# Spreading per-head scalars over partitions: products with a head mask, or 32x32 block transposes

## The chip, the cores and the metric

The kernel runs on one core of a Trainium2 chip. The metric is the device time of the whole program in microseconds (us). The engines are TensorE (PE in the profile; PEld is its weight load), VectorE (DVE), ScalarE (ACT), GpSimd (POOL) and SyncE (SP), each with its own stream of instructions that it runs in order, with waits on semaphores between them.

## The reference, cut to what matters

```python
# x: (64, 32, 512), ctx: (64, 257, 512), 16 heads of 32 columns
x = x + cross_attention(layernorm(x), ctx) @ W_out.T + b_out   # keys = values = ctx
x = x + self_attention(layernorm(x), ...)                      # 16 heads, rope, 32 keys
x = x + moe_ffn(layernorm(x), ...)                             # one of 8 experts a token
# cross attention, for each batch and head:
sim  = q @ k.T * 32 ** -0.5            # 32 queries x 257 keys
out  = softmax(sim) @ v                # = (exp(sim - max) @ v) / sum(exp(sim - max))
```

257 keys are two blocks of 128 and one key more. The kernel takes the two blocks with TensorE and adds the last key by hand: its probability times its value row. It divides by the sums after that, on the attention's result.

## The kernel before, in words

The 64 batches are taken one after the other, each in 11 steps (`STEPS`). Four batches with their 32 queries make a tile of 128 rows; a tile is 44 steps (`TILE`), and there are 16 tiles. Every engine's program is one loop `for step in range(LAST_STEP)`. In a step it issues first its part of the batch now in work (scores, maxima, exponentials, transposes of the probabilities, products with the values, transposes of the next keys), by `step % 11`, and then, in `stages(step)`, the parts of the tiles already past, at the offsets written out by hand at the top of the file. `tile_at(step, offset)` says for which tile a stage is due; offset 0 is the first step after the tile's fourth batch. An offset only fixes the place in the engine's order: the time comes from the waits.

So at each tile boundary (steps 0 to 13 of a tile) work of three tiles meets the first batch `b` of the next one. The order on each engine, by step, is in the kernel before:

- **VectorE**: copy of transposed probabilities of the batch before (step -3), `TURN_K + 1` copies into `k_block` (-2), `X2` add with layernorm statistics of an older tile (1), `largest(b, 0)` and `largest(b, 1)`, the maxima of the scores (2), `SOFT` maximum and subtraction of self-attention (2), `ATT`: last key's product and the sum with `att_bank` (3), `ATT_INV`: product with one over the sums (4), `turn_keys` for `b + 1` (5, 7), `SOFT_SUM` (6), `SOFT_TURN` (12), `largest` of `b + 1` (13), `turn_keys` for `b + 2` (16), `X1` add (17).
- **ScalarE**: `SCALE3`, layernorm of the older tile, which waits for the `X2` statistics (-2), four exponentials of batch `b` (2), `SOFT_EXP` (2), `ATT_HI` (4), copy of transposed probabilities (6).
- **GpSimd**: `PLACE_INV` (-5), `PLACE_LAST` (0), the root for the older tile's layernorm (1), `ATT_LO` (2), `SOFT_SCALE` (4), `keep_last` and `move_last` (7, 9), which place the last key of batch `b + 1`.
- **TensorE**: scores of `b` (0), `attend(b - 1, 1)` and `SELF` (1), `SPREAD` and `SPREAD_INV` (3), `turn_prob(b, 0)` (6), `TURN3` (7), `turn_prob(b, 1)` (8), `attend(b, 0)` (10), `XOUT` in four parts (10 to 13), scores of `b + 1` (11), `attend(b, 1)` (12), `turn_prob(b + 1, 0)` (17), `QKV` (from 24).

The attention result lies in `att_bank` with head dimensions on partitions and the queries of four batches along the columns. The probabilities of the last key (`plast`) and one over the sums (`inv`) lie the other way: a head and a query on a partition, one column for a group of heads and a batch. To bring them over, GpSimd multiplies them into a 0/1 pattern (`latent`), 128x512, and TensorE multiplies four 128x128 blocks of that with a 0/1 mask `samehead`. These results are in two banks of PSUM, which other stages use before and after.

A fp32 product stands as two records in the trace. `XOUT` multiplies operands cut in two (`operand_hi`, `operand_lo`), which `ATT_HI` on ScalarE and `ATT_LO` on GpSimd make from `att_w`.

In the set-up the weights are prepared in units between the first batches. VectorE waits there for a DMA of tables, then copies them, `samehead` among them in 16 copies, at step `TABLES_AT`.

Of the kernel before, what the change touches and what calls it, by code (L numbers as in the profile page):

```python
# [10 lines left out]
P = 128  # L11
# [27 lines left out]
(INVERT, PLACE_LAST, PLACE_INV, X_BIAS, SPREAD, SPREAD_INV, ATT, ATT_INV, ATT_HI, ATT_LO, XOUT, X1, SCALE1, TURN1, QKV, OUT_BIAS, TURN_Q, TURN_K,  # L39
 SELF, SOFT, SOFT_EXP, SOFT_SUM, SOFT_SCALE, SOFT_TURN, SOFT_PLACE, AV, OUT, X2, SCALE3, TURN3, GATE, CHOOSE, RANK,  # L40
 QUERIES) = (
    -5, 0, -5, -6, 3, 3, 3, 4, 4, 2, 10, 17, 19, 21, 24, 26, 41, 41, 45, 46, 46, 50, 48, 56, 55, 63, 83, 89, 86, 95, 105, 105, 118, -54)
# [44 lines left out]
TABLES_AT = 17  # L87
BIAS_LOAD_AT = 8
# [14 lines left out]
def constant_table():  # L103
# [11 lines left out]
        "latent": (p[:, None] % S == np.arange(S)[None, :]),  # L115
        "ofbatch": (p[:, None] // S == np.arange(BT)[None, :]),
# [3 lines left out]
        "samehead": (p[:, None] // HD == p[None, :] // HD),  # L120
# [54 lines left out]
def program(nc, ins, out, const_at, x2_dram, norm3_dram):  # L175
# [37 lines left out]
    ident, latent, rope = const("ident"), const("latent"), const("rope")  # L213
    samehead = sba("samehead", [P, G, HL, HD])
    last_t = sba("last_t", [P, G, B])
# [16 lines left out]
    op_plast = late[:, 5, :].rearrange("p (g b i) -> p g b i", g=G, b=BT)  # L232
# [42 lines left out]
    op_inv = staged_c[:, 0, :].rearrange("p (g b i) -> p g b i", g=G, b=BT)  # L275
# [29 lines left out]
    def pairs(t_):  # L305
# [26 lines left out]
    inverted, plast_placed, inv_placed, spread_done, inv_spread, spread_used, att_added, att_used = (  # L332
        signal(n) for n in ("inverted", "plast_placed", "inv_placed", "spread_done", "inv_spread", "spread_used", "att_added", "att_used"))
# [36 lines left out]
    bank_of = {"queries": 0, "spread": 0, "xout": 0, "norm": 1, "qkv0": 1, "qkv2": 1, "out": 2, "inv": 1, "gate": 0, "av": 0, "qkv1": 2, "q": 1, "k": 0, "norm3": 1, "rank": 0, "qkv3": 0, "self": 1}  # L370
    step_of = {"queries": QUERIES, "spread": SPREAD, "inv": SPREAD_INV, "xout": XOUT, "norm": TURN1, "qkv0": QKV, "qkv1": QKV + 4, "qkv2": QKV + 8, "qkv3": QKV + 12,
# [6 lines left out]
    emptied = {"queries": queries_placed, "spread": spread_used, "inv": att_used, "xout": x1_made, "norm": norm_lo, "q": q2_moved, "self": soft_shifted, "av": self_lo,  # L378
# [26 lines left out]
    def sync_program():  # L405
# [41 lines left out]
        a, b = const_at["latent"][0], const_at["rope"][1]  # L447
        sp.dma_start(consts_1[:, :], ins["const"][:, a:b]).then_inc(tables_loaded, 16)
        a, b = const_at["before"][0], const_at["samehead"][1]
# [39 lines left out]
    def tensor_program():  # L489
# [64 lines left out]
        def attend(b, pair):  # L554
# [5 lines left out]
            for gg in range(2):  # L560
                for c in range(C2):
                    g = 2 * pair + gg
                    for hl in range(HL):
                        place, at, h = hl ^ g, g * P + bl * S, hl * G + g
                        done = pe.matmul(att_bank[hl * HD:(hl + 1) * HD, at:at + S], context[b % 4][:, c, h * HD:(h + 1) * HD],  # L565
                                         prob_t[pair][:, gg, c, place * S:(place + 1) * S], start=(c == 0), stop=(c == C2 - 1))
            done.then_inc(attended, 1)

        def set_up(n):
# [4 lines left out]
            else:  # L574
                until.wait_ge(last_ready, 1)
            if n in units_of_bank[1]:
                until.wait_ge(queries_placed, 2)
            if kind == "xout":
                until.wait_ge(staged_a_loaded, 16)

                for o in range(G):
                    for hl in range(HL):
                        h = hl * G + c
                        done = pe.matmul(bank[hl * HD:(hl + 1) * HD, o * P:(o + 1) * P], staged_a[:, o, h * HD:(h + 1) * HD], ident, start=True, stop=True)
# [21 lines left out]
            if kind == "bias":  # L606
                until.wait_ge(tables_made, 3)
# [9 lines left out]
        def stages(step):  # L617
# [3 lines left out]
            t = tile_at(step, SPREAD)  # L621
            if t >= 0:
                bank = bank_for("spread", t)
                until.wait_ge(tables_made, 3)
# [1154 lines left out]
```

## Time and profile before

| | |
|---|---|
| time, median of 3 runs | 858.45 us (856.07 to 860.0) |
| span of the profiled execution | 854.9 us |
| median less span | 3.55 us |
| busy share of TensorE, VectorE, ScalarE, GpSimd | 90%, 71%, 49%, 37% |
| distance of two boundaries | 36.4 us (15 in 546.5 us, from 70.9 to 617.4) |

The profiled execution has no time of its own beside its span; what lies around the span is taken as the 3.55 us of the table. A busy share is a mean over stages with different limits. An engine that is late at one boundary is late for all that is queued behind it.

### The profile page before, as it was taken

Reading aid. Unit: us, or ns where it says so; the run is one execution under the profiler, and the core shown is the slowest. Engines: PE = TensorE matmul, PEld = TensorE weight load, DVE = VectorE, ACT = ScalarE, POOL = GpSimd, SP = SyncE. Lnnn points to the kernel's source line nnn. Section 1 sums busy time; section 2 is a strip of 40 time slices with the busy share of each in tenths; the row PEclk is TensorE's granted clock in tenths of the full one; section 3 lists DMA queues with packets and bytes.
Section 4 is the critical chain, followed back from the end, with each engine's and each line's share of the span. In section 5 each row is a group of like instructions: output and inputs, shape, how many; then the busy total and the mean of one; then the engine's idle time right before and its main releaser. Section 6 shows DMA issues by size and latency. Waiting matters only on the chain.

```text
span 854.9 us, 26663 instructions
## 1 busy us (share of the span) xinstructions
PE 768.7 (90%) x10666; PEld 577.6 (68%) x10666; DVE 610.8 (71%) x1211; ACT 422.9 (49%) x1062; POOL 313.9 (37%) x638
## 2 busy tenths in 40 slices
PE   4897979989899898988989899898988789999998
PEld 3544767768676786867768676786876556666664
DVE  3477677777877768787777877778645557788883
ACT  2353464554645556464554645546322354555552
POOL 2013533333234242333233234243220435876642
PEclk9999999999999999999999999999999899999999
DMA  9955654656646565484554636564061499454430
GB/s 277 331 130 100 132 153 118 143 140 130 153 112 160 124 162 138 100 184 120 148 142 117 163 110 152 128 159 101 3 222 51 140 375 388 163 172 140 144 115 3
DMA packets 113850, 129.16 MB, mean 151 GB/s; under 512 B 13951, under 2 KB 80767, under 8 KB 113729
## 3 DMA queue, kind: packets, MB, share of 16 engines
q1 hardware_dynamic: 105984, 109.35, 47.7%
q0 software_dynamic: 5520, 16.26, 5.6%
q10 hardware_dynamic: 2224, 1.86, 0.8%
q8 instruction: 85, 1.39, 0.7%
q14 instruction: 37, 0.30, 0.1%
HBM read 114.85 MB, written 14.42 MB: 151 GB/s over the span
## 4 chain that ended last, share of the span: by engine, by line
PE 61%; DVE 16%; POOL 7%; issue 6%; ACT 4%; DMA 3%; SPq 3%; DVEq 0%; POOLq 0%
PE bank L500 10%; PE bank L1560 8%; PE bank L502 8%; PE bank L501 8%; PE bank L494 4%; PE scores L541 3%; PE scores L551 3%; PE bank L565 2%; PE scores L1538 2%; PE scores L1540 2%; PE scores L1539 2%; DVE negmax L1031 2%; PE bank L605 2%; POOL soft L1315 2%; POOL operand_lo L1292 2%
## 5 line engine op out<-in xcount | busy, mean ns | idle before, releaser
L826 ACT ACTIVATE prob<-scores,negmax 128x257 f32<-128x257 f32 x256 | 118.2, 477 | 42.0 <-DVE negmax L1031 41.3
L500 PE MATMUL bank<-qkv_hi,operand_hi 128*128 128x396 f32 x256 | 99.3, 388 | 4.3 <-DVE operand_lo L1035 4.2
L1031 DVE TENSOR_REDUCE negmax<-scores 128x2 f32<-128x514 f32 x128 | 82.1, 683 | 22.2 <-PE scores L541 22.2
L1021 DVE STREAM_TRANSPOSE k_t<-keys 128x512 f32<-128x512 f32 x128 | 88.3, 691 | 5.6 <-DMA keys<-in_ctx 5.5
L501 PE MATMUL bank<-qkv_lo,operand_hi 128*128 128x396 f32 x256 | 88.1, 344 | 0.0
L502 PE MATMUL bank<-qkv_hi,operand_lo 128*128 128x396 f32 x256 | 87.8, 343 | 0.0
L1560 PE MATMUL bank<-w_all,hidden 128*128 x184 | 82.8, 592 | 0.6 <-ACT hidden L1613 0.6
L551 PE MATMUL scores<-consts,prob 128*128 128x128 f32 x512 | 77.6, 276 | 1.6 <-ACT prob L826 1.6
L565 PEld LDWEIGHTS bank<-prob_t,context 128*32 128x32 f32 x4096 | 47.0, 113 | 42.9 <-issue 34.9
L1656 DVE TENSOR_TENSOR w_lo<-w_all,w_hi 128x512 fp32r<-128x512 f32 x89 | 73.3, 882 | 0.2
L551 PEld LDWEIGHTS scores<-consts,prob 128*128 128x128 f32 x512 | 63.2, 144 | 9.6 <-ACT prob L826 2.5
L1026 DVE COPY prob_t<-scores 128x512 f32<-128x512 f32 x64 | 43.0, 672 | 29.4 <-PE scores L551 29.4
L565 PE MATMUL bank<-prob_t,context 128*32 128x32 f32 x4096 | 59.5, 200 | 4.0 <-ACT prob_t L816 3.3
L1560 PEld LDWEIGHTS bank<-w_all,hidden 128*128 128x128 f32 x184 | 34.7, 189 | 35.6 <-issue 33.9
L541 PE MATMUL scores<-k_t,q_t 32*32 32x257 f32 x2048 | 54.0, 395 | 5.4 <-POOL k_t L1265 5.4
L500 PEld LDWEIGHTS bank<-qkv_hi,operand_hi 128*128 128x128 f32 x256 | 48.5, 189 | 13.2 <-DVE operand_lo L1035 6.2
L1592 ACT ACTIVATE w_hi<-w_all 128x512 fp32r (+1 forms) x92 | 54.4, 640 | 5.6 <-PE scores L1540 3.4
L876 ACT ACTIVATE soft_block<-late 32x512 f32<-32x512 f32 x60 | 37.7, 628 | 34.5 <-DVE late L1149 33.4
L826 ACT ACTIVATION_READ_ACCUMULATOR prob<-scores,negmax 128x1 f32 x256 | 52.5, 205 | 0.0
L501 PEld LDWEIGHTS bank<-qkv_lo,operand_hi 128*128 128x128 f32 x256 | 48.8, 191 | 0.0
L502 PEld LDWEIGHTS bank<-qkv_hi,operand_lo 128*128 128x128 f32 x256 | 48.4, 189 | 0.0
L816 ACT ACTIVATE prob_t<-scores 128x512 f32<-128x512 f32 x64 | 37.7, 589 | 15.1 <-PE scores L551 14.7
(249 smaller groups left out, 1705.5 us busy)
## 6 DMA issues: line engine op xcount, KB each, us to landing
keys<-in_ctx SPq DMA_DIRECT2D x256, 128.0 KB, 4.4
context<-in_ctx SPq DMA_DIRECT2D x64, 512.0 KB, 4.6
w_all<-in_L_ffn_W SPq DMA_DIRECT2D x16, 1024.0 KB, 12.3
b<-in_L_ffn_b SPq DMA_DIRECT2D x23, 256.0 KB, 3.6
norm_scratch<-norm SPq DMA_DIRECT2D x16, 256.0 KB, 2.0
x_tile<-in_x SPq DMA_DIRECT2D x8, 256.0 KB, 4.9
x_pair<-in_x SPq DMA_DIRECT2D x8, 256.0 KB, 4.7
x_scratch<-x_tile SPq DMA_DIRECT2D x8, 256.0 KB, 2.5
```

The costliest lines, as they stand in the source:

```text
L500: pe.matmul(to, op_hi[op][:, c, :], w_hi[name][:, c, columns], start=(c == 0), stop=False)
L501: pe.matmul(to, op_hi[op][:, c, :], w_lo[name][:, c, columns], start=False, stop=False)
L502: return pe.matmul(to, op_lo[op][:, c, :], w_hi[name][:, c, columns], start=False, stop=(c == G - 1))
L541: done = pe.matmul(scores[place * S:(place + 1) * S, 2 * pair + gg, 0:J], q_t[rows, 2 * pair + gg, bl, :], k_t[pair][rows, gg, :], start=T ...
L551: done = pe.transpose(scores[:, 2 * pair, at:at + P], prob[pair][:, gg, c * P:(c + 1) * P], ident)
L565: done = pe.matmul(att_bank[hl * HD:(hl + 1) * HD, at:at + S], context[b % 4][:, c, h * HD:(h + 1) * HD], prob_t[pair][:, gg, c, place * S ...
L826: act.activation(prob[pair][:, gg, :], scores[:, g, 0:J], ACT.Exp, bias=negmax[b % 2][:, g:g + 1], accum_out=sums[t % 2][:, g, bl:bl + 1]) ...
L1021: dve.transpose(dst, src).then_inc(keys_turned, 1)
L1031: dve.tensor_reduce(negmax[b % 2][:, 2 * pair:2 * pair + 2], scores[:, 2 * pair:2 * pair + 2, 0:J], AX.X, ALU.max, negate=True).then_inc(m ...
L1560: done = pe.matmul(bank[:, :], hidden[s % 2][:, m, :], w_of[:, bass.ds(place, 1), 1, m, :].rearrange("p a n -> p (a n)"), start=(m == 0), ...
L1592: act.activation(w1_hi[:, k, :], weights[:, k, :], ACT.Copy).then_inc(w1_cut, 1)
L1656: dve.tensor_tensor(w1_lo[:, k, :], weights[:, k, :], w1_hi[:, k, :].bitcast(F32), ALU.subtract).then_inc(w1_low, 1)
```

## The change

The spread is made by VectorE's transpose of 32x32 blocks. Its source is `inv` (or `plast`) with each column repeated 32 times; the transpose turns 32 queries on partitions into 32 columns, the same on all 32 partitions of a head. The two patterns, the masks, the eight products for a tile and their two uses of PSUM banks go. The head order of `att_bank` changes with it (`place` in place of `hl`), and so the weight columns of `XOUT`; the last keys' values are wanted in that order too, as `last_p`, which 16 small products and a ScalarE copy at the start make. The product with the last key's value and the product with one over the sums move from VectorE to GpSimd. Offsets: `SPREAD_INV` -3, `SPREAD_LAST` 0 (both VectorE now), `WEIGH_LAST` 1 and `ATT_INV` 3 (GpSimd), `ATT` from 3 to 2, `ATT_LO` from 2 to 4, `XOUT` from 10 to 8.

```diff
-(INVERT, PLACE_LAST, PLACE_INV, X_BIAS, SPREAD, SPREAD_INV, ATT, ATT_INV, ATT_HI, ATT_LO, XOUT, X1, ...
+(INVERT, SPREAD_INV, SPREAD_LAST, WEIGH_LAST, X_BIAS, ATT, ATT_INV, ATT_HI, ATT_LO, XOUT, X1, ...
-    -5, 0, -5, -6, 3, 3, 3, 4, 4, 2, 10, 17, ...
+    -5, -3, 0, 1, -6, 2, 3, 4, 4, 8, 17, ...
# TensorE, attend
-    done = pe.matmul(att_bank[hl * HD:(hl + 1) * HD, at:at + S], ...
+    done = pe.matmul(att_bank[place * HD:(place + 1) * HD, at:at + S], ...
# TensorE, stages
-            t = tile_at(step, SPREAD)
-            if t >= 0:
-                bank = bank_for("spread", t)
-                until.wait_ge(tables_made, 3)
-                until.wait_ge(plast_placed, t + 1)
-                for g in range(G):
-                    done = pe.matmul(bank[:, g * P:(g + 1) * P], samehead[:, g, :, :].rearrange("p h d -> p (h d)"),
-                                     op_plast[:, g, :, :].rearrange("p b i -> p (b i)"), start=True, stop=True)
-                done.then_inc(spread_done, 1)
-            t = tile_at(step, SPREAD_INV)
...
# TensorE, at the start
+            if step == 0:
+                until.wait_ge(last_ready, 1)
+                turn_last(1)
# VectorE, stages
             t = tile_at(step, INVERT)
...
-                until.wait_ge(inv_placed, t)
...
+            t = tile_at(step, SPREAD_INV)
+            if t >= 0:
+                until.wait_ge(inverted, t + 1)
+                until.wait_ge(att_used, t)
+                until.wait_ge(unit_done, UNITS.index(("bias", 1)) + 1)
+                dve.transpose(over_head(inv_t), per_head(inv)).then_inc(inv_spread, 1)
+            t = tile_at(step, SPREAD_LAST)
+            if t >= 0:
+                until.wait_ge(plast_kept, 2 * BT * (t + 1))
+                until.wait_ge(att_added, t)
+                until.wait_ge(unit_done, len(UNITS))
+                dve.transpose(over_head(last_w), per_head(plast[t % 2])).then_inc(last_spread, 1)
             t = tile_at(step, ATT)
             if t >= 0:
-                until.wait_ge(spread_done, t + 1)
-                until.wait_ge(last_ready, 1)
+                until.wait_ge(last_weighed, t + 1)
                 until.wait_ge(att_hi, t)
                 until.wait_ge(att_lo, t)
-                last = last_t[:, :, BT * t:BT * t + BT].unsqueeze(3).broadcast_to([P, G, BT, S])
-                dve.tensor_tensor(grid4(att_w), grid4(banks[bank_of["spread"]]), last, ALU.mult).then_inc(spread_used, 1)
                 until.wait_ge(attended, 2 * (BT * t + BT))
-                until.wait_ge(spread_used, t + 1)
-                dve.tensor_tensor(att_w[:, :], att_w[:, :], att_bank[:, :], ALU.add).then_inc(att_added, 1)
-            t = tile_at(step, ATT_INV)
-            if t >= 0:
-                until.wait_ge(inv_spread, t + 1)
-                until.wait_ge(att_added, t + 1)
-                dve.tensor_tensor(att_w[:, :], att_w[:, :], banks[bank_of["inv"]][:, :], ALU.mult).then_inc(att_used, 1)
+                dve.tensor_tensor(att_w[:, :], last_w, att_bank[:, :], ALU.add).then_inc(att_added, 1)
+        def per_head(t_):
+            return t_[:, :, :].rearrange("p g b -> p (g b)").unsqueeze(2).broadcast_to([P, G * BT, HD])
+        def over_head(t_):
+            return t_.rearrange("p (n i) -> p n i", i=S)
# VectorE, set-up at TABLES_AT
-                for g in range(G):
-                    for hl in range(HL):
-                        from_ = 2 * P + (hl ^ g) * HD
-                        done = dve.tensor_copy(samehead[:, g, hl, :], tables[:, from_:from_ + HD])
# GpSimd, stages (PLACE_LAST and PLACE_INV go)
+            t = tile_at(step, WEIGH_LAST)
+            if t >= 0:
+                until.wait_ge(last_ready, 2)
+                until.wait_ge(last_spread, t + 1)
+                weight = last_p[:, :, BT * t:BT * t + BT].unsqueeze(3).broadcast_to([P, G, BT, S])
+                pool.tensor_tensor(grid4(last_w), grid4(last_w), weight, ALU.mult).then_inc(last_weighed, 1)
+            t = tile_at(step, ATT_INV)
+            if t >= 0:
+                until.wait_ge(inv_spread, t + 1)
+                until.wait_ge(att_added, t + 1)
+                pool.tensor_tensor(att_w, att_w, inv_t, ALU.mult).then_inc(att_used, 1)
```

## Rows read from the trace of the kernel before

**Rows 1.** The page: span, busy time of each engine, chain that ended last.

```profile
span 854.9 us, 26663 instructions
...
PE 768.7 (90%) x10666; PEld 577.6 (68%) x10666; DVE 610.8 (71%) x1211; ACT 422.9 (49%) x1062; POOL 313.9 (37%) x638
...
PE 61%; DVE 16%; POOL 7%; issue 6%; ACT 4%; DMA 3%; SPq 3%; DVEq 0%; POOLq 0%
```

**Rows 2.** Chain over one boundary: start us, length us, what.

```profile
323.06 0.70 DVE x_tile L1158
...
324.62 1.26 DVE negmax L1031 x2
...
329.42 0.64 ACT operand_hi L837
330.13 0.79 POOL operand_lo L1292
...
331.36 1.05 POOL soft L1315
332.80 0.99 PE scores L541 x32
```

**Rows 3.** Groups by line: product pairs (two records each); busy us, mean ns, idle before.

```profile
L627 PE MATMUL bank<-late,samehead 128*128 128x128 f32 x128 | 18.5, 288 | 1.0 <-POOL late L1281 1.0
L635 PE MATMUL bank<-staged_c,samehead 128*128 128x128 f32 x128 | 18.4, 287 | 10.3 <-DVE soft L1132 10.3
```

**Rows 4.** Timeline of that boundary: start us, us, engine line op [idle before <-releaser].

```profile
320.78 0.69 DVE L1026 COPY prob_t<-scores 128x512 f32<-128x512 f32 x1 [1.27 <-PE scores L551]
...
321.65 1.38 DVE L1122 COPY k_block<-bank 32x512 f32<-32x512 f32 x2 [0.18 <-PE bank L494]
...
324.34 1.10 PE L687 MATMUL bank<-k_block,late 128*32 128x128 f32 x32
...
326.06 0.81 ACT L794 ACTIVATE norm<-x_tile,shift_r,rstd_r 128x512 f32<-128x512 f32 x1 [3.03 <-POOL shift_r L1254]
...
328.72 0.64 ACT L868 ACTIVATE soft<-soft 128x512 f32<-128x512 f32 x1
...
330.58 0.46 PE L565 MATMUL bank<-prob_t,context 128*32 128x32 f32 x32
...
331.55 0.47 PE L500 MATMUL bank<-xout_hi,operand_hi 128*128 128x512 f32 x1 [0.50 <-POOL operand_lo L1292]
...
336.52 0.60 PE L551 MATMUL scores<-consts,prob 128*128 128x128 f32 x4
336.72 0.69 DVE L1075 TENSOR_TENSOR x_pair<-x_pair,bank 128x512 f32<-128x512 f32 x1 [1.24 <-PE bank L502]
...
342.68 0.45 PE L500 MATMUL bank<-qkv_hi,operand_hi 128*128 128x396 f32 x1 [0.30 <-DVE operand_lo L1035]
```

**Rows 5.** Groups by line: the VectorE and GpSimd forms nearest to the new ones.

```profile
L1292 POOL TENSOR_TENSOR operand_lo<-late,operand_hi 128x512 fp32r<-128x512 f32 x16 | 20.4, 1274 | 67.3 <-ACT operand_hi L837 67.3
...
L1287 POOL TENSOR_TENSOR staged_c<-inv,consts 128x512 f32<-128x512 f32 x16 | 16.8, 1050 | 70.8 <-DVE inv L1054 70.8
...
L1149 DVE STREAM_TRANSPOSE late<-soft 128x512 f32<-128x512 f32 x16 | 11.4, 712 | 8.4 <-POOL soft L1315 8.3
...
L1065 DVE TENSOR_TENSOR late<-late,bank 128x512 f32<-128x512 f32 x16 | 11.0, 689 | 1.7
```

**Rows 6.** Timeline of the set-up around the tables.

```profile
36.69 1.46 DVE L1225 COPY samehead<-qk 128x32 f32<-128x32 f32 x16
...
39.13 1.37 PE L584 MATMUL bank<-consts,soft_block 128*32 128x128 f32 x32 [3.88 <-DVE xout_lo L964]
```

**Rows 7.** Stretches: busy us of each engine, then granted clock, DMA share, GB/s.

```profile
39.00:42.00 3.00, 2.87 (x66) 2.29 (x67) 3.00 (x6) 0.60 (x1) 0.00 (x0) 0.63 1.07 178
76.50:82.50 6.00, 5.97 (x76) 3.40 (x77) 3.35 (x7) 1.94 (x8) 1.33 (x4) 0.72 0.24 14
331.50:336.50 5.00, 4.63 (x76) 2.94 (x77) 3.13 (x5) 3.24 (x11) 1.40 (x5) 1.00 0.59 98
```

More of the change, by code:

```diff
@@ L38 @@
 TILE = BT * STEPS
-(INVERT, PLACE_LAST, PLACE_INV, X_BIAS, SPREAD, SPREAD_INV, ATT, ATT_INV, ATT_HI, ATT_LO, XOUT, X1, SCALE1, TURN1, QKV, OUT_BIAS, TURN_Q, TURN_K,
+(INVERT, SPREAD_INV, SPREAD_LAST, WEIGH_LAST, X_BIAS, ATT, ATT_INV, ATT_HI, ATT_LO, XOUT, X1, SCALE1, TURN1, QKV, OUT_BIAS, TURN_Q, TURN_K,
  SELF, SOFT, SOFT_EXP, SOFT_SUM, SOFT_SCALE, SOFT_TURN, SOFT_PLACE, AV, OUT, X2, SCALE3, TURN3, GATE, CHOOSE, RANK,
  QUERIES) = (
-    -5, 0, -5, -6, 3, 3, 3, 4, 4, 2, 10, 17, 19, 21, 24, 26, 41, 41, 45, 46, 46, 50, 48, 56, 55, 63, 83, 89, 86, 95, 105, 105, 118, -54)
+    -5, -3, 0, 1, -6, 2, 3, 4, 4, 8, 17, 19, 21, 24, 26, 41, 41, 45, 46, 46, 50, 48, 56, 55, 63, 83, 89, 86, 95, 105, 105, 118, -54)
 MEASURE_X, SCALE_X = 2 * STEPS + 4, 2 * STEPS + 5
@@ L366, in emptied_unit @@
         return {"down": down_moved, "k": k_summed, "bias": bias_moved}[kind], c + 1
-    bank_of = {"queries": 0, "spread": 0, "xout": 0, "norm": 1, "qkv0": 1, "qkv2": 1, "out": 2, "inv": 1, "gate": 0, "av": 0, "qkv1": 2, "q": 1, "k": 0, "norm3": 1, "rank": 0, "qkv3": 0, "self": 1}
-    step_of = {"queries": QUERIES, "spread": SPREAD, "inv": SPREAD_INV, "xout": XOUT, "norm": TURN1, "qkv0": QKV, "qkv1": QKV + 4, "qkv2": QKV + 8, "qkv3": QKV + 12,
+    bank_of = {"queries": 0, "xout": 0, "norm": 1, "qkv0": 1, "qkv2": 1, "out": 2, "gate": 0, "av": 0, "qkv1": 2, "q": 1, "k": 0, "norm3": 1, "rank": 0, "qkv3": 0, "self": 1}
+    step_of = {"queries": QUERIES, "xout": XOUT, "norm": TURN1, "qkv0": QKV, "qkv1": QKV + 4, "qkv2": QKV + 8, "qkv3": QKV + 12,
                "q": TURN_Q, "k": TURN_K, "self": SELF, "av": AV, "out": OUT, "norm3": TURN3, "gate": GATE, "rank": RANK}
@@ L581, in set_up @@
                 for o in range(G):
-                    for hl in range(HL):
-                        h = hl * G + c
-                        done = pe.matmul(bank[hl * HD:(hl + 1) * HD, o * P:(o + 1) * P], staged_a[:, o, h * HD:(h + 1) * HD], ident, start=True, stop=True)
+                    for place in range(HL):
+                        h = (place ^ c) * G + c
+                        done = pe.matmul(bank[place * HD:(place + 1) * HD, o * P:(o + 1) * P], staged_a[:, o, h * HD:(h + 1) * HD], ident, start=True, stop=True)
             if kind == "down":
@@ L606, in set_up @@
             if kind == "bias":
-                until.wait_ge(tables_made, 3)
+                until.wait_ge(tables_made, 2)
                 for k in range(2):
@@ L928, in scalar_program @@
                 load_low()
+            if step == LAST_PLACED_AT:
+                until.wait_ge(last_turned, 2)
+                act.activation(last_p[:, :, :].rearrange("p g b -> p (g b)"), last_bank[:, G * B:2 * G * B], ACT.Copy).then_inc(last_ready, 1)
             if step == BIAS_LOAD_AT:
```

69 lines of the change are left out of this document (23 added, 46 removed).

## The prediction

> **What bounds the kernel now.** I read the page first. It shows TensorE 90% busy and the chain that ended last with only 61% of the span on it [rows 1]. So there are stretches in which TensorE's order waits for the others, and the question is whether the change works in these or in TensorE's own. The groups by line price what goes: the two groups of spreading products have 128 records each, eight in a tile [rows 3]. The chain in order of time places it: from 323.06 to 332.80 us, the boundary between two tiles, it runs over VectorE (`X2` add, statistics, the two maxima, self-attention's maximum and subtraction, the three `ATT` operations), then `ATT_HI`, `ATT_LO`, `SOFT_SCALE`, and back to TensorE with the scores of batch b + 1 [rows 2]. TensorE's own work does not set that stretch. From 342.68 on, when `QKV` starts, it is TensorE's products again. The timeline of the same boundary [rows 4] gives starts and waits. Here VectorE has next to no gap: 1.27 us before the copy at 320.78, 0.18 us before the copies at 321.65, then work without a wait until past 330 us. The boundaries lie 36.4 us apart (the table), so I work out one and count.
>
> **What goes.** On TensorE, eight products a tile, in two groups. Their records overlap, so the busy time counts: 18.5 and 18.4 us over 16 tiles, 1.16 us a group and 2.3 us a tile [rows 3]. To that comes the wait of the second group for the bank that `SOFT` empties, 10.3 us in all, 0.7 in each of 15 boundaries. They are due between the end of `SELF` at 325.44 and `turn_prob(b, 0)`, which waits for exponentials. These start after ScalarE's layernorm at 326.06, which waits 3.03 us for `X2`'s statistics [rows 4]; the four exponentials take from 326.87 to 328.72, 0.46 us each, so two are done at 327.8. The removed products stand in a hole of TensorE that stays; I value them at nothing in the steady boundaries. The bank wait of `TURN3` goes too, and also lies there. GpSimd loses 1.05 us twice, at times when it waits.
>
> **What is added on VectorE.** Before: three operations of 0.69 us, all behind the maxima and `SOFT`. After: two transposes, and one addition of 0.69. A transpose whose source repeats a column is not in the trace. The nearest row is the 128x512 transpose of 0.71 us [rows 5], and I take that. Bounds: 0.25 us a transpose if only the 16 distinct columns counted (my guess at a floor: a third of the row), 1.4 us if the source were taken at half the rate, twice the row. VectorE's total for a tile is the same, but the order isn't. The transpose of `inv` (step -3) stands before the `k_block` copies and finds a gap of 0.18 us, so they come 0.52 us later. The one of `plast` (step 0) stands before the `X2` add and finds none: 0.73 us with its pitch. So `X2` starts at 324.31, not 323.06: 1.25 us later, with the statistics, GpSimd's root, ScalarE's layernorm, the maxima and the exponentials behind it. The addition (step 2) now stands before `SOFT`; VectorE is back at its old time with `turn_keys(b + 1, 0)`, 329.3.
>
> **ScalarE's part.** In the kernel before, two paths ended together at `ATT_HI`: VectorE's third `ATT` operation and ScalarE's `SOFT_EXP`, which ended at 329.36 just before `ATT_HI` at 329.42 [rows 2, 4]. From the layernorm to there ScalarE is without a gap for 3.3 us. The change shortens the first path but shifts the second by the whole 1.25 us, so `ATT_HI` starts at 330.67 and `ATT_LO` at 331.38.
>
> **GpSimd's part.** `WEIGH_LAST` has one operand repeated like `PLACE_INV`: 1.05 us; `ATT_INV` has two full ones like `ATT_LO`: 1.27 us [rows 5]. `WEIGH_LAST` runs from 324.35 to 325.4: the root's statistics come at 325.95 and the addition at 327.15, so it is hidden, with 0.5 us to spare. `ATT_INV` runs from 327.9 to 329.2 and `ATT_HI` is held by ScalarE to 330.67: hidden, 1.4 us to spare. Without that cover it would cost 0.58 us more than on VectorE. The row has 1.27 us on GpSimd for what takes 0.69 on VectorE. The Trainium skill says the same in GPSIMD Reference, Engine selection: elementwise work belongs on VectorE, as GpSimd is about twice as slow with two inputs. By that rule alone the boundary would lose another 0.6 us; by the rows it is cover that decides. `SOFT_SCALE`, `keep_last` and `move_last` are queued behind `ATT_LO`, and come 1.25 us later.
>
> **XOUT earlier in the order.** `ATT_LO` releases `XOUT` at 332.8 (331.55 before). Two of its parts now stand before `attend(b, 0)`, whose operand had been there since about 332, and three before the scores of b + 1. Before, `attend(b, 0)` filled the wait at 330.58, and the stretch from the first part to `turn_prob(b + 1, 0)`, 331.55 to 336.52, held four parts, one `attend` and the scores [rows 4]. After, it holds one `attend` more, 0.46 us of products and some 0.3 of issue, less the 0.3 us that the scores waited for `move_last`: `turn_prob(b + 1, 0)` comes at 338.2. The scores of b + 1 start at about 335.8, not 332.8; VectorE begins their two maxima when the first pair is there, some 0.8 us later (all take 0.99 [rows 2]); the maxima take 1.26, a key transpose 0.7 like the one in [rows 5], and only then comes `X1`, at 338.5. It started at 336.72. From `X1` the chain runs to `QKV` at 342.68 as before. So one boundary costs 1.8 us, of which 1.25 by the transposes' place and 0.5 by the order of `XOUT`. `QKV` and what follows is TensorE's, without slack to win it back.
>
> **The sum.** Thirteen boundaries (t = 2 to 14) have all this work: 13 x 1.8 = 23.4 us. t = 1 has no `X2` behind the transposes: 1.3. The last has no next batch, and only the shift on the way to its `ATT_HI`: 0.8. At t = 0 there is nothing of older tiles: 0. In the set-up the 16 copies, 1.46 us, stand between the tables' landing and the product at 39.13, which waited 3.88 us for them [rows 6]: -1.5. The added 16 products and copy at the start lie before that landing, which waits for nobody's compute: 0. Sum +24.0: a span of 878.9 and, with the 3.55 us around it, 882.5 us. The profiled execution stands for the median, as the table has them.
>
> **The rivals.**
> TensorE is left without work from 325.44 to about 329.1, and again for 1.5 us before `XOUT`. After a wait of 3.88 us in the set-up its granted clock was 0.63 for 3 us, part of it thus at 1.2 GHz [rows 6, 7]. The same stretch of `XOUT`, scores and attends took 6.0 us at 0.72 and 5.0 at 1.00 [rows 7]: 1.0 us more a boundary, 13 us, 895 us. The spreading products had kept TensorE at work there, which speaks for it; against it, the slow time may fall in the second hole. The Trainium skill, TensorE: Matmul & The Clock Gate, Part 1, has the rule that the gate halves the clock after idleness and gives it back after activity. By that rule this rival is the forecast; the traces bear it out in the set-up only. Chance 0.2.
> The transposes are cheap: at 0.25 us, 0.07 + 0.25 and half of the order's 0.5, 0.6 us a boundary: 13 x 0.6 - 1.5 + 1 = +7, 866 us. Chance 0.1.
> No change: their cost is paid by TensorE's relief in parts that I value at nothing, about 858. Chance 0.08.
> The other side: it is TensorE's order that holds the boundary, and the earlier steps only move waits. Then each of 15 boundaries gives 2.3 us of products back, with the set-up 36 us: 822. It decides if the exponentials of b are ready before the removed products would have ended; the 3.03 us wait of the layernorm speaks against it. Chance 0.12, at any size.
> The forecast has 0.5. With transposes at 1.4 us it is 3.1 a boundary, 899.
>
> **Range and chances.** 864 to 899 holds the forecast with its bounds, the clock and the cheap transposes, 0.8. Under 0.5%, 4.3 us, this measurement can't tell from no change. Faster 0.12, same 0.08, slower 0.8. The likeliest's own range is 874 to 890.
>
> **What would show it.** Right: `X2` starts 1.2 us later after the last `out` product; the layernorm's wait on ScalarE grows to over 4 us; a hole of 3.7 us on TensorE before `turn_prob(b, 0)` and one before `XOUT`; `XOUT` still waits for `operand_lo`; boundaries 38.2 us apart, at granted clock 1.00. Wrong: boundaries nearer than 36.4, transposes far from 0.71, a granted clock under 1.00 in the steady part, or GpSimd as what ends VectorE's or ScalarE's waits.

## The result, and the profile after

The changed kernel takes 898.21 us, median of 4 runs (893.85 to 903.07); the kernel before took 858.59 us in 4 runs beside it (856.07 to 860.0). The ratio is 1.0467, interval 1.0418 to 1.0516: slower, by 39.6 us. The forecast was 882.5 us, with a range to 899: the result lies 0.8 us under the end of the range, and outside of the likeliest's own range (874 to 890). The profiled execution took 901.93 us, near the slow end of the four, so the spans below differ by more than the medians, by 45.1 us. Executions that took over 1.5% longer than the fastest of the same kernel are left out of all medians, ranges and ratios here (one of six and two of ten, in two of the experiments).

The page of the changed kernel, lines that answer to [rows 1], and between them TensorE's granted clock in the 40 slices of the span:

```profile
span 900.0 us, 26139 instructions
...
PE 773.6 (86%) x10442; PEld 573.5 (64%) x10442; DVE 604.1 (67%) x1195; ACT 422.1 (47%) x1063; POOL 319.6 (36%) x638
...
PEclk9998898989898898989889898988989889999999
...
PE 55%; DVE 14%; issue 10%; POOL 8%; ACT 7%; SPq 3%; DMA 2%; ACTq 0%; POOLq 0%; DVEq 0%
```

TensorE has 224 instructions fewer than in [rows 1] and is busy 5 us longer: what is left takes longer. Its share of the chain fell from 61 to 55%. The mean granted clock of the execution is 0.926, and the low slices lie all through the steady part.

The same boundary as in [rows 4] (here tile by tile earlier in time, as `X2` at 302.62 us shows), in the timeline of the changed kernel:

```profile
299.88 0.70 DVE L1049 STREAM_TRANSPOSE staged_c<-inv 128x512 f32<-128x512 f32 x1
300.51 1.34 DVE L1114 COPY k_block<-bank 32x512 f32<-32x512 f32 x2
...
301.10 0.40 PE L499 MATMUL bank<-out_hi,operand_lo 128*128 128x512 f32 x1
...
301.88 0.71 DVE L1055 STREAM_TRANSPOSE late<-plast 128x512 f32<-128x512 f32 x1
...
302.62 0.69 DVE L1150 TENSOR_TENSOR x_tile<-x_tile,bank 128x512 f32<-128x512 f32 x1
302.67 1.05 POOL L1273 TENSOR_TENSOR late<-late,last_p 128x512 f32<-128x512 f32 x1 [6.13 <-DVE late L1055]
...
302.83 1.09 PE L667 MATMUL bank<-k_block,late 128*32 128x128 f32 x32
...
305.62 0.81 ACT L781 ACTIVATE norm<-x_tile,shift_r,rstd_r 128x512 f32<-128x512 f32 x1 [4.10 <-POOL shift_r L1248]
...
306.18 1.27 POOL L1278 TENSOR_TENSOR late<-late,staged_c 128x512 f32<-128x512 f32 x1 [0.59 <-DVE late L1062]
...
307.53 1.11 PE L548 MATMUL scores<-consts,prob 128*128 128x128 f32 x4 [3.61 <-ACT prob L813]
...
308.79 0.63 ACT L824 ACTIVATE operand_hi<-late 128x512 fp32r<-128x512 f32 x1
...
309.50 1.28 POOL L1283 TENSOR_TENSOR operand_lo<-late,operand_hi 128x512 fp32r<-128x512 f32 x1 [2.06 <-ACT operand_hi L824]
...
310.83 0.79 PE L497 MATMUL bank<-xout_hi,operand_hi 128*128 128x512 f32 x1 [0.48 <-POOL operand_lo L1283]
...
314.78 0.80 PE L538 MATMUL scores<-k_t,q_t 32*32 32x257 f32 x32
...
317.38 0.65 DVE L1067 TENSOR_TENSOR x_pair<-x_pair,bank 128x512 f32<-128x512 f32 x1
```

The two transposes take 0.70 and 0.71 us. TensorE's last `OUT` product ends at 301.50 and `X2` starts at 302.62, 1.12 us later, since the second transpose stands before it; in the kernel before this is 0.04 us. The layernorm waits 4.10 us (3.03 in [rows 4]). `ATT_INV` on GpSimd (306.18, 1.27 us) ends at 307.45, and `ATT_HI` starts at 308.79: it is covered. `SELF` ends at 303.92, and TensorE then waits 3.61 us for an exponential. The stretches of that boundary (busy us of TensorE, its weight loads, VectorE, ScalarE and GpSimd, then the granted clock, DMA share and GB/s, as in [rows 7]):

```profile
302.00:306.00 4.00, 1.92 (x96) 1.24 (x80) 3.90 (x8) 0.38 (x1) 2.11 (x4) 1.00 0.01 4
306.00:309.00 3.00, 1.47 (x7) 1.47 (x8) 2.00 (x5) 2.97 (x11) 1.27 (x1) 0.57 0.67 187
309.00:312.00 3.00, 2.52 (x10) 1.92 (x9) 2.23 (x5) 1.40 (x3) 2.50 (x5) 0.50 0.99 257
312.00:315.00 3.00, 3.00 (x56) 1.90 (x70) 0.53 (x1) 1.26 (x2) 0.28 (x3) 0.80 0.48 80
315.00:318.00 3.00, 2.50 (x71) 1.34 (x54) 2.45 (x4) 1.72 (x8) 0.00 (x0) 1.00 0.07 16
```

In and after the hole the granted clock is 0.57, 0.50 and 0.80: TensorE has fallen from 2.4 to 1.2 GHz. `XOUT`'s first product takes 0.79 us there (0.47 in [rows 4]); the scores of b + 1 start 12.16 us after `X2` and take 0.80 us, at full clock again.

Where the time went, by the starts of `X2` in the two traces. `X2` of the oldest tile comes at 140.26 before and 145.89 after: +5.6. The 13 distances from there to the last such `X2` sum to 474.89 before (140.26 to 615.15) and 512.52 after (145.89 to 658.41): +37.6, 2.9 a boundary. What follows is 1.9 longer. One distance is 42.90, with a stop that the last section tells of; the other 12 have a mean of 39.1, where the mean was 36.5 before.

### The profile page after: what moved, and what is told of

It reads as the page before. It is cut to its first block, busy times and chain, and to the rows that moved or that the text cites. A ratio compares the mean times of both kernels' runs of the same rounds, so it can differ in the third digit from the quotient of the medians.

```text
span 900.0 us, 26139 instructions
## 1 busy us (share of the span) xinstructions
PE 773.6 (86%) x10442; PEld 573.5 (64%) x10442; DVE 604.1 (67%) x1195; ACT 422.1 (47%) x1063; POOL 319.6 (36%) x638
## 3 DMA queue, kind: packets, MB, share of 16 engines
q1 hardware_dynamic: 105984, 109.26, 46.6%
## 4 chain that ended last, share of the span: by engine, by line
PE 55%; DVE 14%; issue 10%; POOL 8%; ACT 7%; SPq 3%; DMA 2%; ACTq 0%; POOLq 0%; DVEq 0%
PE bank L497 11%; PE bank L498 8%; PE bank L499 8%; PE bank L1551 7%; PE scores L548 3%; PE scores L538 3%; PE bank L562 3%; PE bank L491 3%; ACT prob L813 2%; POOL operand_lo L1283 2%; DVE k_block L1114 2%; PE scores L1529 2%; PE scores L1531 2%; PE scores L1530 2%; PE bank L602 2%
## 5 line engine op out<-in xcount | busy, mean ns | idle before, releaser
L548 PE MATMUL scores<-consts,prob 128*128 128x128 f32 x512 | 89.5, 303 | 60.7 <-ACT prob L813 60.7
L548 PEld LDWEIGHTS scores<-consts,prob 128*128 128x128 f32 x512 | 67.5, 156 | 73.4 <-ACT prob L813 68.1
L1647 DVE TENSOR_TENSOR w_lo<-w_all,w_hi 128x512 fp32r<-128x512 f32 x89 | 69.5, 839 | 0.1
L562 PE MATMUL bank<-prob_t,context 128*32 128x32 f32 x4096 | 61.4, 202 | 1.9 <-issue 1.9
L497 PE MATMUL bank<-xout_hi,operand_hi 128*128 128x512 f32 x64 | 40.7, 635 | 15.4 <-POOL operand_lo L1283 15.4
L863 ACT ACTIVATE soft_block<-late 32x512 f32<-32x512 f32 x60 | 37.7, 628 | 34.1 <-DVE late L1141 33.0
L1265 POOL COPY plast<-prob 128x2 f32<-128x2 f32 x128 | 25.0, 195 | 78.6 <-ACT prob L813 78.6
L538 PE MATMUL scores<-k_t,q_t 32*32 32x257 f32 x2048 | 51.9, 394 | 0.8 <-POOL k_t L1259 0.8
L1273 POOL TENSOR_TENSOR late<-late,last_p 128x512 f32<-128x512 f32 x16 | 16.8, 1050 | 98.9 <-DVE late L1055 98.9
```

The lines of the kernel that those rows point to most:

```text
L497: pe.matmul(to, op_hi[op][:, c, :], w_hi[name][:, c, columns], start=(c == 0), stop=False)
L538: done = pe.matmul(scores[place * S:(place + 1) * S, 2 * pair + gg, 0:J], q_t[rows, 2 * pair + gg, bl, :], k_t[pair][rows, gg, :], start=T ...
L548: done = pe.transpose(scores[:, 2 * pair, at:at + P], prob[pair][:, gg, c * P:(c + 1) * P], ident)
L562: done = pe.matmul(att_bank[place * HD:(place + 1) * HD, at:at + S], context[b % 4][:, c, h * HD:(h + 1) * HD], prob_t[pair][:, gg, c, pla ...
L1647: dve.tensor_tensor(w1_lo[:, k, :], weights[:, k, :], w1_hi[:, k, :].bitcast(F32), ALU.subtract).then_inc(w1_low, 1)
```

## The experiments

All are edits of the changed kernel, but one of the kernel before. Ratios are to the kernel before, run on the same chip beside them. The changed kernel itself was not run again there, so what an experiment gains on it is given as a difference of medians across chips, where the medians of the kernel before lie within 2 us of each other (857.64 to 859.54). "Distance" is that from one `X2` to the next in the one profiled execution, for the same 13 boundaries.

**The order of `XOUT` alone put back** (`XOUT` 8 to 10, so `attend(b, 0)` and the scores of b + 1 stand before its parts as they did).

```diff
-    -5, -3, 0, 1, -6, 2, 3, 4, 4, 8, 17, ...
+    -5, -3, 0, 1, -6, 2, 3, 4, 4, 10, 17, ...
```

> The changed kernel with XOUT back at step 10, so that attend(b, 0) and the scores of b + 1 again stand before its parts two to four; the transposes stay. Theory (place of the transposes 1.25 us, order of XOUT 0.5 us, clock the rest of the 2.9 us a boundary): the order's share comes back, 0.5 to 1.0 us in 13 boundaries, 885 to 892 us, and the clock still falls in the hole before turn_prob(b, 0). Rival (the order of XOUT is what costs, since it holds back the next scores): 865 or less. Rival (order costs nothing once the clock is down): 898.

Measured: 875.62 us, ratio 1.0226 (1.0192 to 1.0260); 22.6 us less than the changed kernel, where the forecast's step had 0.5 a boundary, 6.5 in all. It is between the theory and its rival, and neither holds. Distances are 37.4 to 37.5 in six of 13 tiles, 37.6 to 38.8 in the others; the mean clock rose to 0.949. The clock still fell in every tile, but in nine of them for a shorter time. By the two profiles, 21.3 us of the gain are in the 13 boundaries and 3.8 before the first `X2`. So the order matters more than its products' time at full clock: what it costs and what the clock costs are not separate.

**TensorE's hole filled**: seven products of 256 columns, of constants into a free bank, before `turn_prob(b, 0)`. Their results are used by nobody; nothing else changes.

```diff
# TensorE, stages
+            t = tile_at(step, 3)
+            if 1 <= t:
+                until.wait_ge(qkv_moved, 4 * (t - 1) + 4)
+                for _ in range(7):
+                    pe.matmul(banks[0][:, 0:FILL], ident, consts[:, 0:FILL], start=True, stop=True)
```

> The changed kernel with seven products of 256 columns without use, issued by TensorE at step 3 of each tile from the second on, about 3 us of work in the hole of 3.6 us before turn_prob(b, 0). Theory (the clock falls in that hole and costs 1.0 to 1.3 us a boundary): granted clock 1.00 to 0.98, boundaries 38.2 to 38.4 us apart, 883 to 887 us, although work is added. Rival (the clock falls where it costs nothing and the loss is all late VectorE and ScalarE work): 898 or more.

Measured: 878.79 us, ratio 1.0264 (1.0231 to 1.0297), 19.4 less than the changed kernel (17 to 19 when each is taken against the kernel before beside it), by added work. That is lower than the theory had it. The timeline of a boundary and its stretches:

```profile
215.64 0.69 DVE L1155 TENSOR_TENSOR x_pair<-x_pair,bank 128x512 f32<-128x512 f32 x1
...
216.87 3.29 PE L622 MATMUL bank<-consts 128*128 128x256 f32 x14
...
218.64 0.81 ACT L786 ACTIVATE norm<-x_pair,shift_r,rstd_r 128x512 f32<-128x512 f32 x1 [4.10 <-POOL shift_r L1253]
...
220.55 0.66 PE L548 MATMUL scores<-consts,prob 128*128 128x128 f32 x4 [0.39 <-ACT prob L818]
...
223.85 0.50 PE L497 MATMUL bank<-xout_hi,operand_hi 128*128 128x512 f32 x1 [1.73 <-POOL operand_lo L1288]
```

```profile
216.50:220.50 4.00, 3.66 (x31) 2.75 (x22) 3.93 (x8) 1.84 (x6) 2.56 (x5) 1.00 0.06 20
220.50:223.50 3.00, 1.57 (x12) 1.27 (x12) 1.99 (x5) 2.92 (x8) 0.97 (x1) 1.00 1.00 336
223.50:226.50 3.00, 2.65 (x41) 1.88 (x41) 1.30 (x3) 0.90 (x2) 1.80 (x6) 1.00 0.83 165
```

The hole before `turn_prob(b, 0)` is down to 0.39 us and the clock stays at 1.00. Up to `XOUT` VectorE's, GpSimd's and ScalarE's part is the same to the hundredth (the layernorm again 3.00 us after `X2` and again 4.10 us late), `XOUT` starts 8.21 us after `X2` in both, and `X1` comes 13.7 after it instead of 14.6 to 15.7. The distance is mostly 37.70 (37.67 to 37.88 in eleven tiles); in the two others, of 38.86 and 41.01, the clock fell later in the tile. This run shows the clock's share by itself: some 1.4 us a boundary, 17.8 us in the 13 of them by the two profiles.

**The transpose of `inv` moved to VectorE's gap** (step -3 to -4, where VectorE waits 1.26 us for transposed probabilities before the copy).

```diff
-    -5, -3, 0, 1, -6, 2, 3, 4, 4, 8, 17, ...
+    -5, -4, 0, 1, -6, 2, 3, 4, 4, 8, 17, ...
```

> The changed kernel with the transpose of one over the sums one step earlier (-4), before the copy for which VectorE waited 1.27 us. Theory (its place behind that copy made X2 0.52 us later): X2 starts 0.5 us earlier, 7 us in all, 889 to 892 us with the clock as it is; if the shorter hole also keeps the clock, 880. Rival (a transpose's place does not matter): 898.

Measured: 883.08 us, ratio 1.0302 (1.0242 to 1.0363). The time from the last `OUT` product to `X2` falls from 1.11 to 0.80 us, so this transpose costs 0.31 us there, not the 0.52 of the forecast. The time is under the theory's 889 to 892 and over its 880 for a clock that is kept. Distances are 37.39 in two tiles at clock 1.00, 37.0 to 37.4 in four at 0.95, and 38.4 to 39.5 in six at 0.91; one of 39.29 at clock 1.00 has a stop that the last section tells of. That 0.95 can cost nothing is answered under "Its size" below.

**Both transposes in the gap, and `XOUT`'s order put back** (both at -4; for the first tile `plast`'s stays at step 0).

```diff
-    -5, -3, 0, 1, -6, 2, 3, 4, 4, 8, 17, ...
+    -5, -4, -4, 1, -6, 2, 3, 4, 4, 10, 17, ...
             t = tile_at(step, SPREAD_LAST)
+            if t == 0:
+                t = -1
+            if step == TILE:
+                t = 0
```

> The changed kernel with both transposes at step -4 (for the first tile the last key's stays at step 0, where its buffer comes free), and XOUT back at step 10. Theory (the loss is the place of the transposes, with the clock and the order behind it): X2 starts right after its product as in the kernel before, no hole over 2.5 us, clock near 1.00, boundaries 36.2 to 36.8 us apart, 853 to 864 us. Rival (GpSimd's two products on the way from ATT to ATT_LO cost by themselves): ATT_HI waits for GpSimd, 870 or more.

Measured: 870.63 us, ratio 1.0161 (1.0132 to 1.0190). All that VectorE and the order had lost is given back, and it is still slower than before. The theory (853 to 864 us, clock near 1.00) failed; the rival named 870 or more, but by another cause: `ATT_HI` follows `SOFT_EXP` on ScalarE, 1.4 us after its operand is ready at 259.93, and does not wait for GpSimd. A boundary in the timeline, TensorE's part, and its stretches:

```profile
255.11 0.69 DVE L1154 TENSOR_TENSOR x_pair<-x_pair,bank 128x512 f32<-128x512 f32 x1
...
260.02 0.66 PE L548 MATMUL scores<-consts,prob 128*128 128x128 f32 x4 [2.56 <-ACT prob L813]
...
264.90 1.24 PE L538 MATMUL scores<-k_t,q_t 32*32 32x257 f32 x32
```

```profile
262.00:264.00 2.00, 1.33 (x34) 1.10 (x35) 1.52 (x4) 0.90 (x2) 2.00 (x2) 0.50 1.04 332
264.00:266.00 2.00, 2.00 (x35) 0.61 (x33) 0.71 (x1) 0.92 (x2) 0.78 (x5) 0.50 0.79 137
```

`X2` starts 0.05 us after the last `OUT` product's end, as before. The hole is 2.56 us now, and the clock falls to 0.50: the scores of b + 1 take 1.24 us instead of 0.80. Distances are 36.35 and 36.37 in two of 13 tiles and 37.2 to 38.0 in the others, 37.51 as a mean. Against the 36.33 that the same kernel reaches with its hole filled (below), the clock alone costs 1.2 us a boundary, and 1.3 to 1.7 in ten of the tiles.

**The removed products' width, in the kernel before**: each spreading product takes 8 columns instead of 128, so that it spreads only the first 8 columns; the last key's share and the division are taken from old values elsewhere. Order and waits stay.

```diff
-                    done = pe.matmul(bank[:, g * P:(g + 1) * P], samehead[...
-                                      op_plast[:, g, :, :].rearrange("p b i -> p (b i)"), start=True, stop=True)
+                    done = pe.matmul(bank[:, g * P:g * P + 8], samehead[...
+                                      op_plast[:, g, :, :].rearrange("p b i -> p (b i)")[:, 0:8], start=True, stop=True)
```

> The kernel before with its spreading products 8 columns wide in place of 128 (the rest of the two banks is not written by them, so the last key's share and the division use stale values): nearly all of TensorE's spreading work goes and every wait, transposes and order stay as they were. Theory (those products kept the clock up): the clock falls below 1.00 at the boundaries, which get 0.5 to 1.3 us longer, 865 to 876 us. Rival (they are cover that nobody needs; the clock falls only in the longer hole of the changed kernel): 855 to 859, clock 1.00 in the steady part. Rival (TensorE's order held the boundary): 835 or less.

Measured: 867.01 us, ratio 1.0103 (1.0067 to 1.0140): narrower products in the kernel before make it 8.1 us slower. The edit takes less away than the expectation says. The weight loads stay, and a group is still busy 16.9 us over 16 tiles, where it was 18.5 [rows 3]:

```profile
L627 PE MATMUL bank<-late,samehead 128*128 128x8 f32 x128 | 16.9, 258 | 1.0 <-POOL late L1281 1.0
```

The distances are 36.1 to 36.5 in seven tiles and 36.8 to 36.9 in six, and the clock is 1.00 in three tiles only, 0.95 in the others. One boundary:

```profile
221.00:224.00 3.00, 2.27 (x28) 2.01 (x18) 2.86 (x5) 2.20 (x8) 0.64 (x2) 1.00 0.18 71
224.00:227.00 3.00, 2.36 (x45) 1.78 (x43) 2.86 (x6) 2.67 (x8) 1.16 (x1) 0.80 1.03 309
227.00:230.00 3.00, 2.86 (x47) 1.52 (x38) 1.66 (x4) 1.08 (x2) 1.62 (x6) 0.63 0.83 149
230.00:233.00 3.00, 3.00 (x45) 2.05 (x43) 2.06 (x4) 2.67 (x10) 0.00 (x0) 1.00 0.32 71
```

So the clock does hang on these products: with most of their columns gone it fell at ten of 13 boundaries, where it never fell before, and the mean clock of the four executions is 0.945 to 0.953, against 0.98 or more in all 15 of the kernel before beside them. But that costs little there, 0.3 us in six of them and 1.6 over all 13, not the 0.5 to 1.3 a boundary of the theory, whose 865 to 876 us came out by other parts. The first `X2` comes at 145.36, 5.1 us later than before, of which 1.35 are there at 72 us, before the first edited product runs; what follows the last of the 13 is 2.3 us longer, and there the old values may also choose other experts for the tokens. How much of the 8.1 us is the products' doing is therefore not shown. In the changed kernel, where the hole has no product in it at all, the steady part costs far more.

**The order put back and the hole filled** (the first two experiments together).

```diff
-    -5, -3, 0, 1, -6, 2, 3, 4, 4, 8, 17, ...
+    -5, -3, 0, 1, -6, 2, 3, 4, 4, 10, 17, ...
...
+                for _ in range(7):
+                    pe.matmul(banks[0][:, 0:FILL], ident, consts[:, 0:FILL], start=True, stop=True)
```

> The changed kernel with the seven products without use in its hole and XOUT back at step 10: both of the edits that were tried alone. Alone the order gave 23 us and the filling 19 us. Theory (the order of XOUT costs nothing at full clock; its 23 us were slow products put before the next scores, and the clock itself): same as the filling alone, boundaries 37.6 to 37.8 us, 876 to 880. Rival (the order has a cost of its own): the gains add up, boundaries 37.2 or less, 870 or less.

Measured: 870.33 us, ratio 1.0132 (1.0107 to 1.0158), distance 37.42 at clock 1.00 (two tiles have 38.0). Against the filled kernel with the new order, 37.70, the order costs 0.28 us in a usual tile at full clock, 3.6 us over 13. The medians differ by more, 8.5 us, which speaks for the rival (870 or less). In the profiles the rest lies in the two long tiles of the kernel with the new order, 38.86 and 41.01 us.

**Both transposes in the gap, order back, hole filled** (with five products, as the hole is shorter; the edit for the first tile as above).

```diff
-    -5, -3, 0, 1, -6, 2, 3, 4, 4, 8, 17, ...
+    -5, -4, -4, 1, -6, 2, 3, 4, 4, 10, 17, ...
...
+                for _ in range(5):
+                    pe.matmul(banks[0][:, 0:FILL], ident, consts[:, 0:FILL], start=True, stop=True)
```

> Both transposes in VectorE's gap (step -4), XOUT at step 10, and five products of 256 columns without use at step 3, for the shorter hole of 2.56 us. Theory (what was left of the loss with the transposes in the gap is the clock: its boundaries that were undisturbed came at 36.36 us): clock 1.00, boundaries 36.3 to 36.4 us, 853 to 858 us. Rival (something else of the 1.2 us a boundary stays): 865 or more.

Measured: 853.96 us in 5 runs (849.13 to 855.98), ratio 0.9934 (0.9905 to 0.9964): faster than before, by 0.7%, and as the theory had it. Distances are 36.3 to 36.7, mostly 36.33, at clock 1.00 in nine of 13 tiles and 37.2 to 37.7 at 0.95 in four. Against 37.42, the transposes' place costs 1.09 us.

**The same with `ATT_HI` ahead of `SOFT_EXP` on ScalarE** (4 to 2), the diff against the kernel just above.

```diff
-    -5, -4, -4, 1, -6, 2, 3, 4, 4, 10, 17, ...
+    -5, -4, -4, 1, -6, 2, 3, 2, 4, 10, 17, ...
```

> The kernel with both transposes in the gap and the hole filled, and besides ATT_HI at step 2, before SOFT_EXP on ScalarE. With the transposes in the gap ATT_HI's operand is there 0.8 us before ScalarE has done the exponentials, so only the order holds it. Theory: ATT_LO and XOUT come 0.6 us earlier, SOFT_SCALE about as before, boundaries 35.8 to 36.2 us, 846 to 853 us, faster than the kernel before. Rival (SOFT_EXP, one place later, holds SOFT_SUM, SOFT_SCALE and the next batch's last key as long): no difference.

Measured: 857.85 us in 8 runs (851.11 to 862.87), ratio 0.9971 (0.9940 to 1.0002): no difference from before is shown. In the profiled execution, one of 862.87 us, the distance is 36.07 to 36.13 at clock 1.00 in the first five tiles, then 37.54 to 37.68 at 0.95 in the next seven: 0.2 us won a boundary, and more given back by the clock.

**The same with two more such products before `attend(b, 0)`, with `ATT_HI` at 2 and at 4.**

```diff
+            if tile_at(step, 9) >= 1:
+                for _ in range(2):
+                    pe.matmul(banks[0][:, 0:FILL], ident, consts[:, 0:FILL], start=True, stop=True)
```

> As the kernel with both transposes in the gap, the hole filled and ATT_HI before SOFT_EXP, with two more products of 256 columns at step 9, in TensorE's wait of 0.87 us before attend(b, 0). With the first hole alone filled, the boundaries came at 36.1 us at clock 1.00 and at 37.6 at 0.95, and stayed at the one or the other. Theory (the second hole decides between them): all boundaries at 36.1 us and clock 1.00, 845 to 851 us, faster than the kernel before by 1% or so. Rival (the gate's phase decides, a filled second hole changes nothing): a spread of 850 to 870 again.

> The same with ATT_HI back at step 4, after SOFT_EXP. Theory: clock 1.00 at all boundaries, 36.33 us each, so 0.2 us a boundary slower than with ATT_HI first, 848 to 854 us. Rival: as above, a spread of 850 to 865.

Measured: with `ATT_HI` at 2, 851.71 us in 7 runs (849.02 to 857.34), ratio 0.9919 (0.9890 to 0.9948); at 4, 857.97 us in 12 runs (853.14 to 861.51), ratio 0.9981 (0.9960 to 1.0002). Both are over their theories (845 to 851 and 848 to 854), though in both profiles the clock is 1.00 at all 13 boundaries, as the theories said. A boundary of the first:

```profile
285.01 2.43 PE L622 MATMUL bank<-consts 128*128 128x256 f32 x10
...
288.36 0.64 ACT L832 ACTIVATE operand_hi<-late 128x512 fp32r<-128x512 f32 x1
...
288.88 0.64 ACT L863 ACTIVATE soft<-soft 128x512 f32<-128x512 f32 x1
...
289.02 1.03 PE L625 MATMUL bank<-consts 128*128 128x256 f32 x4
...
290.44 0.50 PE L497 MATMUL bank<-xout_hi,operand_hi 128*128 128x512 f32 x1
```

Its distance is 36.1 in nine tiles, 0.4 less than before, and 36.4 to 36.9 in four (the mean is 36.25). Its median is the lowest: the changed kernel's idea, with places and fill of its own, beats the kernel before by 0.8%. Whether it is faster than the kernel with five products and `ATT_HI` at 4 (0.9934) is not shown, since the intervals overlap. The second has 36.35 in nearly all tiles; in its profiled execution the span is 851.3, but its median is not lower than that of the kernel without the two products (853.96). What the two do in the executions that no profile shows stays open.

## Why the prediction was right or wrong

The forecast's sign and most of its mechanism held. What failed is a term that the sum left out, the granted clock. That the time still falls within the range is luck: its upper end, 899, was the price of transposes twice as long, which did not happen, and the time is 3 us over the 895 of the clock's rival. Of the signs of being right, the boundaries 38.2 us apart at clock 1.00 did not come (39.1 at 0.91); that of being wrong, a granted clock under 1.00 in the steady part, did.

| term, us a boundary | forecast | measured | from |
|---|---|---|---|
| place of the two transposes | 1.25 | 1.1 | 37.42 less 36.33; 1.07 by `OUT`'s end to `X2` |
| order of `XOUT`, at full clock | 0.5 | 0.28 in a usual tile; 0.65 by medians | 37.70 less 37.42; 8.5 us over 13 |
| all else, products gone | 0 | -0.2 | 36.33 less the 36.53 before |
| clock | not in the sum; rival, 1.0 | 1.4 | 39.1 less 37.70; 17 to 19 us in all |

- **Place.** The transposes cost what the nearest row had (0.702 and 0.711 us as means of 16). `plast`'s came out at 0.75 us (0.80 less the 0.05 with both in the gap), forecast 0.73; `inv`'s at 0.31 instead of 0.52. `WEIGH_LAST` 1.05 and `ATT_INV` 1.27 us on GpSimd were hidden as forecast. The Trainium skill (GPSIMD Engine Reference, Engine selection) has such work on VectorE, since GpSimd is about twice as slow with two inputs. The factor agrees with 1.27 against the 0.69 us that [rows 5] have for such an operation on VectorE; under cover it decided nothing here.
- **Removed products worth nothing.** Right for their own time, wrong for what they did to TensorE. The forecast saw the hole and its length (3.7, measured 3.61), and had written that the products "had kept TensorE at work there"; then it set the clock aside as a rival of chance 0.2, because the slow time might fall into the second hole. This is the step that failed. The slow time did not fall in the second hole: it covered part or all of `turn_prob`, and most or all of `XOUT`'s parts that stand before the scores of b + 1. The second hole was 0.48 us in seven tiles, because slower products before it filled it, and 0.97 to 1.45 in six, where 1.5 had been expected (TensorE's wait, from 145 to 640 us, with total us, times, longest):

```profile
PE bank L497 <- POOL operand_lo L1283: 11.2, 13, 1.4
```

- **Its size.** 1.0 a boundary came from one stretch at 0.72 against one at 1.00 [rows 7]. `X1` comes 14.64 to 14.89 us after `X2` in one tile and 15.43 to 15.70 in the next, against 13.7 with the hole filled: the first kind costs 1.0 to 1.2, near the forecast's rival, the second 1.7 to 2.0, in turn. The granted clock tells them apart. It is low for as long in both, but from 3.8 us after `X2` in the tile of 302.62 us and only from 6 us after it in that of 341.40 us, so that more of the slow time falls on `XOUT`'s parts, behind the longer second hole (the two tiles, at the same times after `X2`):

```profile
306.40:308.40 2.00, 0.87 (x4) 0.87 (x5) 1.54 (x3) 1.97 (x10) 1.04 (x1) 0.50 0.56 209
313.20:315.20 2.00, 2.00 (x69) 1.14 (x67) 0.00 (x0) 0.63 (x1) 0.00 (x0) 0.99 0.06 9
345.20:347.20 2.00, 0.89 (x8) 0.86 (x8) 1.51 (x3) 1.98 (x10) 1.01 (x1) 1.00 0.59 217
352.00:354.00 2.00, 2.00 (x36) 1.36 (x35) 0.00 (x0) 0.61 (x1) 0.00 (x0) 0.50 0.09 19
```

The experiments show the same. A shorter low stretch that begins 4.3 to 5.4 us after `X2` cost nothing in two of them: 37.4 us with `inv`'s transpose moved, as at clock 1.00, and 36.35 with both transposes in the gap, where 36.33 is the distance with the hole filled. One as short that begins 9.4 to 10.0 us after `X2`, over the scores of b + 1, cost 1.3 to 1.6 us.
- **The order of `XOUT`.** In a usual tile at full clock half of the forecast, since VectorE and the last key's moves on GpSimd follow faster than assumed (scores of b + 1 at 11.1 us after `X2`, forecast 11.5). At low clock it is the dearer part: the slow `XOUT` parts stand before the scores that VectorE waits for. Put back alone, it gave 22.6 us.
- **The start.** The forecast had -1.5 for the set-up copies and +1.3 for the first full boundary, together nothing before the first `X2`. With the hole filled that `X2` is at 140.25, before at 140.26: right as a sum in that execution. The copies gave what was forecast: from the start of VectorE's first work on the landed tables to the product that waited [rows 6] it is 1.28 us in the changed kernel, 2.65 before. But the tables landed later, by 0.4 to 2.1 us in the profiles (38.59 in the changed kernel's own, 36.48 before). The first maxima come at 14.99 instead of 13.49, behind the 16 products and ScalarE's copy at the start, which the forecast had at no cost. Of the +5.6 to the first `X2`, 4.0 are there by 109.26 us, where the maxima of batch 8 start (105.31 before, 105.09 with the hole filled). The filling products first run at 105.5 us, so it isn't they that spare these 4.0. The granted clock from 80 to 100 us is 0.80, against 0.90 before and 0.91 in the filled kernel; that this is the cause is argued, not shown.

Summed: the filled kernel is 21.2 us over the kernel before beside it, where the forecast had 24.0, so without the clock it was 3 us high; the clock added 17 to 19. [rows 6, 7] had shown a fall once, at a wait of 3.88 us, and the new hole was forecast at 3.7. The Trainium skill has the rule (TensorE: Matmul & The Clock Gate, Part 1) that the array halves its clock when it has idled and gets it back by being busy. The traces bear it out behind the holes of 3.61 and 2.56 us, at 0.50; but with `ATT_HI` early the clock fell as well behind waits of at most 0.87 us.

The other side fell: `turn_prob(b, 0)` was held by the exponentials in every boundary, as the waits of TensorE in the changed kernel show (total us, times, longest):

```profile
PE scores L548 <- ACT prob L813: 53.1, 26, 3.6
```

That is, from 145 to 640 us, 53.1 us of waiting in 26 waits, two at each of 13 boundaries: one of about 3.6 us before `turn_prob(b, 0)` and one of 0.5 before `turn_prob(b + 1, 0)`. Cheap transposes fell with their 0.7 us, and no change with the interval.

What the runs leave open: what sets the time at which the clock falls in a tile, and in which executions of one kernel it falls.

## What to carry to other kernels

Work taken from an engine that waits anyway can still be worth its time: before pricing it at nothing, add up TensorE's hole without it, look in the trace for a hole of that length, and price the half clock behind it over the products that the next waits hang on. Where the low stretch falls decides its price: here from nothing to 2.0 us a boundary. A repeated-column transpose costs what a plain one costs; its place in VectorE's order is what decides, and there it belongs where VectorE waits already, not before an add that others are behind. If a hole can't be closed by useful work, a few products whose result nobody reads can be tried in it: they held no other engine up here and gave 17 to 19 us.

## What the runs showed of the hardware that was not expected

- **The clock fell after a hole of 2.56 us too.** That is the kernel with both transposes in the gap; at the boundary shown it was at 0.50 from 262 to 266 us, for longer than the hole. It was still 1.00 in the hole and fell 1.2 us after its end (260.02), with TensorE at work again. With five products in the hole and 0.19 us of it left, it stayed at 1.00 in nine tiles.
- **It fell without such a hole too.** With `ATT_HI` early and the first hole filled, TensorE's longest waits between 316 and 332 us are 0.87 and 0.64 us, and the clock was 0.51 from 331.7 to 335.2. Two products in the wait of 0.87 us, and it was 1.00 at all 13 boundaries of that profile.
- **The clock keeps a pattern.** In the kernel with `ATT_HI` early, boundaries are 36.1 us apart at clock 1.00 for five tiles, then 37.55 at 0.95 for seven, with the same instructions. Executions of that kernel take 851.11 to 862.87 us; that this spread is the same pattern with other shares of the two kinds is argued, not shown, as only one was profiled.
- **A stop of TensorE inside a group.** In the changed kernel's longest tile:

```profile
362.22 0.41 PE L562 MATMUL bank<-prob_t,context 128*32 128x32 f32 x25
364.58 0.33 PE L562 MATMUL bank<-prob_t,context 128*32 128x32 f32 x7 [1.95 <-issue]
```

The other 25 of the 32 products had run, and the profile names no wait of the last seven: the stop is put down to issue. It takes 2.0 of the 3.8 us by which that tile is longer than the mean of the others, and the clock falls again behind it (to 1.2 GHz at 364.4 us). Such a stop is found once in each of the three profiles with `XOUT` at step 8: in this one, of 2.0 us in the kernel with the hole filled (distance 41.0), and of 2.05 us in the one with `inv`'s transpose moved (39.29). Of those with `XOUT` at 10, only the last experiment's has one, of 1.34 us (37.53). No cause was found.
